# A fused two-block network on one core: the attention stage's 48 slots written out, against a hardware loop of three turns over twelve of them

## The reference

```
x = x + ga * mixer0(layernorm(x) * (1 + ca) + sa)        # a recurrence over tokens
x = x + gb * experts0(layernorm(x) * (1 + cb) + sb)      # one of 8 experts for each token
x = x + ga * attention1(layernorm(x) * (1 + ca) + sa)    # 3 layers, see below
x = x + gb * tiles1(layernorm(x) * (1 + cb) + sb)        # one of 8 matrices for each position
```

```
q, k, v = out @ Wq + bq, out @ Wk + bk, out @ Wv + bv
Qf, Kf  = features(q), features(k)                 # exp of a projection, both signs
a       = causal sum over tokens: Qf (Kf^T v) / (Qf sum Kf)
h       = layernorm(out + a @ Wo + bo)
out     = layernorm(h + relu(h @ W1 + bf1) @ W2 + bf2)
```

## Time and profile before

| what | value |
|---|---|
| median of three runs | 2030.56 us (2025.53 to 2031.26) |
| the profiled execution, its own time | 2030.56 us |
| span of that execution, first to last instruction | 2028.7 us |
| PE busy | 1673.9 us (83%) |
| DVE busy | 1552.6 us (77%) |
| POOL busy | 981.9 us (48%) |
| ACT busy | 882.8 us (44%) |
| attention stage on PE, first to last slot's L1568 | 629.5 to 1814.9 us |

### The profile page before, as it was taken

How to read it: one execution, slowest core, us unless ns; L and a number is a source line. 1 busy time by engine, 2 the same in 40 slices (tenths; PEclk the granted TensorE clock), 3 DMA queues, 4 the chain that set the end, 5 groups by cost and what they waited for, 6 DMA issues and landing times. The chain is left out here.

```text
span 2028.7 us, 67977 instructions
## 1 busy us (share of the span) xinstructions
PE 1673.9 (83%) x28443; PEld 1255.2 (62%) x28445; DVE 1552.6 (77%) x3835; ACT 882.8 (44%) x1642; POOL 981.9 (48%) x1045
## 2 busy tenths in 40 slices
PE   5655555459946999999999999999999999996798
PEld 4333334359944666666666666666666666663798
DVE  2899964459975878878788788778878888885675
ACT  2555555446622444444444444444444444442321
POOL 0677747769953324324334334234324334333797
PEclk9877765579977999999999999999999999997899
DMA  7400001122230000000000000000000000000001
GB/s 207 84 0 0 0 23 33 36 61 64 63 119 1 3 3 3 3 3 3 3 3 3 3 3 3 3 3 3 3 3 3 3 3 3 3 3 1 16 31 37
DMA packets 60715, 42.75 MB, mean 21 GB/s; under 512 B 19720, under 2 KB 54800, under 8 KB 59952
## 3 DMA queue, kind: packets, MB, share of 16 engines
q1 hardware_dynamic: 47504, 25.35, 4.8%
q0 software_dynamic: 4352, 8.99, 1.3%
q10 hardware_dynamic: 8608, 4.67, 0.9%
HBM read 24.22 MB, written 14.77 MB: 19 GB/s over the span
## 5 line engine op out<-in xcount | busy, mean ns | idle before, releaser
L368 POOL TENSOR_TENSOR at_rstd<-at_mv,const 128x4 f32<-128x4 f32 x96 | 19.4, 202 | 555.9 <-DVE at_mv L362 555.9
L1612 PE MATMUL psum<-attn_w,at_qa 128*128 128x128 f32 x1536 | 184.1, 278 | 0.0
L1604 PE MATMUL psum<-at_vT,attn_w 128*128 128x512 f32 x384 | 179.8, 611 | 1.7 <-ACT at_vT L1417 0.9
L1612 PEld LDWEIGHTS psum<-attn_w,at_qa 128*128 128x128 f32 x1536 | 175.2, 192 | 2.6 <-issue 0.5
L1421 ACT ACTIVATE at_qa<-psum,attn_bf 128x512 f32<-128x512 f32 x192 | 131.9, 687 | 89.3 <-PE psum L1604 89.3
L1316 DVE TENSOR_SCALAR at_kb<-at_kf,const 128x512 f32<-128x512 f32 x192 | 157.8, 881 | 0.0
L1322 DVE STREAM_TRANSPOSE at_vb<-at_vT 32x512 uint32<-32x512 uint32 x192 | 134.7, 701 | 1.9
L1838 PE MATMUL psum<-tilesT,ti_masked 128*128 128x128 f32 x1024 | 120.0, 279 | 13.0 <-POOL ti_masked L1800 13.0
L1838 PEld LDWEIGHTS psum<-tilesT,ti_masked 128*128 128x128 f32 x1024 | 117.9, 195 | 14.6 <-issue 14.6
L1546 PE MATMUL psum<-at_state,at_qa 64*64 64x36 f32 x3072 | 115.7, 242 | 8.1 <-issue 7.1
L1425 ACT ACTIVATE at_qa<-at_qf,const 128x512 f32<-128x512 f32 x192 | 122.2, 710 | 0.0
(11 more groups left out here) (303 smaller groups left out, 4306.8 us busy)
## 6 DMA issues: line engine op xcount, KB each, us to landing
ex_xs<-sorted_x SPq DMA_DIRECT2D x80, 65.0 KB
x<-in_L_attn_x ACTq DMA_DIRECT2D x8, 512.0 KB, 7.7
ex_feats<-token_y SPq DMA_DIRECT2D x4, 1024.0 KB, 8.0
out<-x SPq DMA_DIRECT2D x16, 256.0 KB, 2.3
expert_w<-in_L_ffn_w SPq DMA_DIRECT2D x1, 2048.0 KB, 9.0
attn_w<-in_L_attn_W SPq DMA_DIRECT2D x2, 768.0 KB
token_y<-ex_y,ex_place POOLq DMA_INDIRECT x72
sorted_x<-ex_spare SPq DMA_DIRECT2D x1, 1040.0 KB, 7.2
```

The lines of the kernel that those rows point to most:

```text
L1604: mm(bank(f.s, c), k.w1[:, f.l, c * P:(c + 1) * P], hT[f.s][:], start=True, stop=True).then_inc(hid_ready, 1)
L1612: last = mm(bank(f.s, 1)[:, c * D:(c + 1) * D], hidden[f.s][:, t, c * P:(c + 1) * P], k.w2[:, f.l, t, :], start=(t == 0 and c == 0), stop= ...
```

## The change

Slots 11 to 46 (36 of the 49 entries that `slots` yields) come from a hardware loop of three turns whose body is 12 slots. The first eleven entries and the last two stay written out. `turn` inside the loop is the loop's counter, so wait numbers, batch and chunk numbers, and the base of `Steps` are worked out from it in registers while the kernel runs. The work of each slot and its order are as before. All five engines' programs go through `slots` except SP's, which has no part in this stage.

```
             yield layer_at(0, 0), None, layer_at(1, 0)
-            for i in range(1, BODY * PAIRS - 1):
+            for i in range(1, BODY - 1):
                 yield trio(i, 0)
-            last, after_it = (layer_at(BODY * PAIRS - i, 0) for i in (2, 1))
+            before = st.k if st else 0
+            with eng.Fori(0, PAIRS - 1) as turn:
+                if st:
+                    st.begin(turn, before)
+                for i in range(BODY - 1, 2 * BODY - 1):
+                    yield trio(i, turn)
+                if st:
+                    st.end()
+            if st:
+                st.begin(PAIRS - 1, before)
+            last, after_it = (layer_at(BODY - i, PAIRS - 1) for i in (2, 1))
             yield after_it, last, None
             yield None, after_it, None
```

## The result

The changed kernel took 2046.86 us, median of 4 runs (2045.37 to 2049.01), beside 2030.91 us for the kernel before on the same chip (4 runs, 2025.53 to 2032.21). The ratio is 1.0091, 95% interval 1.007 to 1.0111: slower by 0.9%. The forecast was 2045 us, slower by 0.7%. The profiled execution took 2053.53 us itself, so its trace has some 7 us more than the median; the second trace, of `after_again`, is of an execution of 2043.50 us and is set beside it where it matters. Lines behind the diff are ten higher: L1568 of before is L1578 here.

The account below looks back on a forecast made before the run. The prediction took the attention stage to be bound by PE. Branches 7.6, alignment 4 and ScalarE 2.6 us summed to 14.2 us on 2030.6, so 2045 us; forecast 2037 to 2056 us, 8-in-10 range 2033 to 2060 us.

Parts of the forecast that it names:

- Arithmetic: In the attention stage's slots, nothing in the order or size of the work changes: 0 us.
- The way back, twice: At the loop's two taken branches, PE waits for an unrequested code block: 3.8 us each, 7.6 us in all.
- Alignment of blocks: In the looped slots, all turns share the same fetch-block boundaries and lose 36.5 us against 32.5: +4 us.
- Registers: Wait values worked out in registers on PE, DVE and POOL are covered by other work: 0 us.
- ScalarE: At the head of layer 0, two slices by a register add 0.22 us in 12 slots: 2.6 us.
- Sum: All terms together: 14.2 us on 2030.6, so 2044.8, called 2045 us, slower by 0.7%.
- Turns near 307 to 309 us: Sign in the profile after: the loop's three turns of equal length, 307 to 309 us with the way back.
- code that stays: Rival: PE keeps the loop's body, so turns two and three have no fetch pauses: 2009 to 2014 us, 4 in 100.
- register work: Rival: register work reaches PE in the slots, 0.5 to 1.1 us a slot: 2059 to 2085 us, 12 in 100.
- the way back that costs nothing: Rival: branch target fetched ahead, or good alignment pays for it: 2030 to 2036 us, within 0.3%, 17 in 100.
- Costs far more: Rival: each way back takes two fetches in a row on PE, then DVE, 10 us a turn: 2056 to 2060 us, 9 in 100.

Follow-up runs that it names:

- after_again: The changed kernel measured once more, nothing altered, with more rounds: 2045.22 us (6 runs), ratio 1.0087 to the kernel before.
- no_back: The changed kernel with the 36 looped slots written out again, `turn` still in a register, so no branch is taken: 2030.4 us, ratio 1.0019 to the kernel before.
- one_back: The changed kernel with the first of three turns written out and a loop over the other two, one taken branch left: 2042.42 us, ratio 1.0078.
- pads: The kernel before, written out, with 94 NOPs in each PE slot, placed by hand in three portions: 2019.83 us, ratio 0.9977.
- fixed_gain: The changed kernel with layer 0's gain and bias always read from batch 0's columns, so no slices by a register there: 2039.92 us, ratio 1.0061.
- hold5: The kernel before, no branch, with PE held at the first product of five slots until SyncE made four small transfers each: 2060.44 us, ratio 1.0162.
- pause: The kernel before, no branch, with PE held at the start of two slots until SyncE made two small transfers each: 2031.12 us, ratio 1.0026.
- loop_pads: The changed kernel with the closing branch's target announced at each turn's top and NOPs padding each PE slot (87 in looped slots): 2032.83 us, ratio 1.004.
- hint: The changed kernel with the closing branch's target announced to every engine's fetcher at the top of each turn: 2047.51 us, ratio 1.0105.
- pause3: The kernel before, no branch, with PE held at the start of two slots until SyncE made three small transfers each: 2033.76 us, ratio 1.005.

## Why the prediction was right, step by step

- *Arithmetic*: 0, held; the counts are equal.
- *The way back, twice*: the step that was mis-sized. Held: the code is gone, one block is waited for (3.73 and 3.88 us against 3.8), and no second fetch pause follows. Missed: the granted clock of 0.50 behind the wait, 2.55 and 3.1 us in the first trace, 1.2 and 2.5 in the second. Forecast 7.6 us, measured 13.4 and 11.4 by the two traces. The prediction put the clock at nothing and gave no reason, though the line at 729.77 above stands right behind one of its own. The section "Instruction fetch mechanics" of the Trainium skill's page "Runtime: NRT & Kernel Launch" says that a taken branch to absent code forces a fetch before execution goes on; the 3.73 us agree. It has no price, and names no clock.
- *Alignment of blocks*: the excess over 36 clean slots was 32.5 us before. After it is 51.1, less 13.4 for branches and 0.1 to 1.5 for ScalarE: 36.2 to 37.6, so +3.7 to +5.1 against +4. The second trace gives 47.2 - 11.4 less the same, +1.8 to +3.2, and `no_back` +4.3 in its trace and 4 us in time. The size held, but partly by luck: `one_back` shows +7 for another placement, `pads` -7.5. Nor is the excess all fetches, as the prediction had it: of the 32.5 us, 24.7 are pauses by "issue" in those slots, the rest waits for other engines and the lower clock. (3 x 12.2 is 36.6, not 36.5, which changes nothing.)
- *Behind the exit*: not in the sum at all, as it counted only the 36 looped slots; 2.6 us measured.
- *Registers*: 0 on PE, held; clean slots of 24.34 us, and `no_back` leaves no room for more. (This rival's price should have begun at 2045 + 18 = 2063 us, not 2059.)
- *ScalarE*: 2.6 us forecast in 12 slots; its direct part is 0.1 to 1.5 us. L1408 is late by 0.26 us, about as forecast; the cover I called thin held in most slots, as the second half of the weighed part, with its fetch pause, was still running (932.65 us above).
- *Sum*: 14.2 us forecast, 16 to 18 us measured. The branches were 4 to 6 us too low and the exit 2.6, and ScalarE 1 to 2.5 us too high, so the total is low by 2 to 4 us, inside its range. The mechanism was right; that the number came this near owes something to the luck with the placement and to errors of opposite sign. Turns near 307 to 309 us: they were 307.4, 310.1 and 309.5, the way back and the lower clock falling into different turns.
- *Rivals*: code that stays is out by 210 packets; register work by the clean slots; the way back that costs nothing by `no_back`. "Costs far more" was near in kind: two blocks do move around the way back (from 1209.35 and 1211.32), but the first before the branch is taken, so only one wait shows, and the clock makes up the rest.

## What to carry to other kernels

A hardware loop whose body is too long to stay on the engine is no saving at run time: here each way back costs one exposed block fetch of 3.6 to 4.05 us on the busiest engine, and 1.2 to 3.1 us more by the clock behind it, 5 to 7 us in all; behind the exit another 1 to 2.7 us went, by the three traces. So price an idle gap on TensorE at more than its length: look in the timeline at the wide products right behind it, which show the lower level by nearly doubling. When small products make up the run, write down instructions and not only work: a block of 256 that passes in less than the fetch takes leaves PE idle, and where the boundaries fall is worth several microseconds in either direction without any other change.

## What the runs showed of the hardware

- The granted clock was 0.50 for some 3 to 6 us of work behind idle stretches of 3.60 to 4.05 us at seven ways back (two each in both traces of the change and in `fixed_gain`, one in `one_back`) and of 2.76 to 4.08 us at the five holds of `hold5`. Behind 1.93 us it fell in `pause`, behind 1.92 and 1.90 in `loop_pads`, behind fetch pauses of 1.78 and 1.21 us in the kernel before. It did not fall behind 1.88, 2.26 and 2.52 us in `hint`, 2.88 us in `pause3`, or 1.80 us at 906.50 in the change. Length alone does not decide it, and these runs don't say what else does.
- NOPs on PE that nothing covers cost about 0.05 us each (5.0 us for some 94); 94 a slot in three portions behind and between wide products cost nothing that shows.
- A back-edge hint about halves the wait at the branch (3.73 and 3.88 us to 1.88 and 2.26) and makes the code behind the exit late (2.52 us).
- Without any branch, 36 slots of straight-line code had 24.7 us of fetch pauses and took 32.5 us more than 36 clean slots; the hand-padded kernel still took 25.0 us more (300.42 + 300.25 + 300.22 us by its windows, less 875.9).
